# Choosing the next step by its later phases too, and the first batch ahead of the second, in a planned four-layer diffusion-transformer kernel

## What is computed

```python
# layer 0: self-attention with a 1024x1024 mask, rope; layer 1: no mask; layer 3: rope, no mask
# layer 2: self-attention in windows of 128 tokens, rolled by 64
for layer in (0, 1, 2, 3):
    h = modulate(layernorm(x), cond)                    # all tokens of a batch
    q, k, v = heads(h @ w_qkv)
    x = x + gate * (softmax(q @ k.T * 0.25 (+ mask)) @ v @ w_o + b_o)
    h = layernorm(x)                                    # modulated, but in layer 1
    q = h @ w_cross_q;  k, v = heads(ctx @ w_kv)        # 77 keys
    s = q @ k.T * 0.25                                  # layer 2: only the 16 largest scores of a row count
    x = x + gate * (softmax(s) @ v @ w_co + b_co)
    h = modulate(layernorm(x), cond)
    x = x + gate * (act(h @ w1 + b1) @ w2 + b2)         # gelu; in layer 2 silu(h @ a) * (h @ b)
```

## Time and profile before

| | us |
|---|---|
| median of 3 runs | 3243.97 (3241.6 to 3250.75) |
| the profiled execution | 3256.22 |
| its span, first to last instruction | 3254.4 |
| PE busy | 2751.2 (85%) |
| DVE busy | 1942.0 (60%) |
| ACT busy | 1529.2 (47%) |
| POOL busy | 669.2 (21%) |
| mean granted TensorE clock | 0.888 |

### The profile page before, as it was taken

How to read it: one execution, slowest core, us unless ns; L and a number is a source line. 1 busy time by engine, 2 the same in 40 slices (tenths; PEclk the granted TensorE clock), 3 DMA queues, 4 the chain that set the end, 5 groups by cost and what they waited for, 6 DMA issues and landing times.

```text
span 3254.4 us, 44342 instructions
## 1 busy us (share of the span) xinstructions
PE 2751.2 (85%) x13324; PEld 1246.8 (38%) x13376; DVE 1942.0 (60%) x4404; ACT 1529.2 (47%) x2744; POOL 669.2 (21%) x970
## 2 busy tenths in 40 slices
PE   5899999897889999998889774657688999997788
PEld 3433343224452423223546552334323523232545
DVE  6787566243458687752443567756997278873421
ACT  2055646553535575675353442323244374676242
POOL 4010100212411111112241334433312000112020
PEclk9699999888789999998889886768889999998878
DMA  5412112212441332133264652210412023124220
GB/s 182 132 55 64 47 50 83 81 35 85 125 121 44 92 113 63 51 96 101 77 178 116 190 165 74 74 32 27 127 37 52 17 63 101 47 76 127 80 92 17
DMA packets 254274, 275.88 MB, mean 85 GB/s; under 512 B 60485, under 2 KB 195424, under 8 KB 253664
## 3 DMA queue, kind: packets, MB, share of 16 engines
q1 hardware_dynamic: 242783, 271.58, 28.4%
q0 software_dynamic: 11264, 1.46, 0.3%
HBM read 157.36 MB, written 114.09 MB: 83 GB/s over the span
## 4 chain that ended last, share of the span: by engine, by line
PE 68%; DVE 13%; issue 7%; ACT 4%; DMA 4%; POOL 3%; SPq 1%; ACTq 0%; DVEq 0%; POOLq 0%
PE ring_a L1207 10%; PE ring_c L1281 10%; PE ring_b L1251 10%; PE ring_b L1304 7%; PE ring_a L1316 7%; PE ring_b L1166 4%; PE ring_a L1293 4%; PE ring_b L1250 3%; DVE row_max L1547 2%; ACT probs L1385 2%; PE ring_b L1275 2%; PE ring_b L1132 2%; PE ring_a L1180 2%; PE ring_a L1304 2%; DVE x_norm L1464 1%
## 5 line engine op out<-in xcount | busy, mean ns | idle before, releaser
L1385 ACT ACTIVATE probs<-ring_b 128x512 f32<-128x512 f32 (+1 forms) x1728 | 913.3, 600 | 569.3 <-PE ring_b L1251 469.8
L1547 DVE TENSOR_REDUCE row_max<-ring_a 128x1 f32<-128x1024 f32 x512 | 600.3, 1219 | 105.2 <-PE ring_a L1207 101.9
L1251 PE MATMUL ring_b<-q_ring,k_ring 100*128 100x512 bf16 x1536 | 525.5, 387 | 36.4 <-ACT probs L1385 22.8
L1207 PE MATMUL ring_a<-k_ring,q_ring 96*128 96x512 bf16 x1536 | 492.8, 410 | 45.8 <-DVE row_max L1547 20.2
L1281 PE MATMUL ring_c<-probs,v_and_ones 128*17 128x512 f32 x3072 | 410.0, 606 | 3.4 <-ACT probs L1385 3.4
L1665 POOL CAST neg_max_parts<-neg_max 16x128 bf16<-16x128 f32 x112 | 35.6, 318 | 1804.0 <-ACT neg_max L1379 1476.7
L1544 DVE CUSTOM_DVE_ANT_0 w_mlp<-ring_a,w_mlp 128x1024 bf16<-128x1024 f32 x256 | 304.1, 1222 | 82.9 <-PE ring_a L1207 80.0
L1591 DVE TENSOR_TENSOR x_tok<-x_tok,ring_a 128x512 f32<-128x512 f32 x96 | 66.0, 687 | 413.8 <-PE ring_a L1316 260.1
L1207 PEld LDWEIGHTS ring_a<-k_ring,q_ring 96*128 96x128 bf16 x1536 | 125.9, 100 | 405.4 <-issue 333.9
L1251 PEld LDWEIGHTS ring_b<-q_ring,k_ring 100*128 100x128 bf16 x1536 | 146.7, 99 | 312.4 <-issue 207.2
L1304 PE MATMUL ring_b<-h_feat,w_mlp 128*128 128x512 f32 x512 | 247.6, 633 | 8.7 <-ACT h_feat L1350 8.6
(11 more groups left out here) (138 smaller groups left out, 3319.3 us busy)
## 6 DMA issues: line engine op xcount, KB each, us to landing
q_ring<-scr_q SPq DMA_DIRECT2D x128, 384.0 KB, 4.0
scr_q<-split SPq DMA_DIRECT2D x64, 384.0 KB, 3.1
k_ring<-scr_k SPq DMA_DIRECT2D x64, 384.0 KB, 4.8
scr_q<-split SPq DMA_DIRECT2D x64, 256.0 KB, 3.2
scr_out<-out_stage SPq DMA_DIRECT2D x128, 128.0 KB, 2.5
scr_out<-out_stage SPq DMA_DIRECT2D x64, 256.0 KB, 2.0
h_feat<-scr_out SPq DMA_DIRECT2D x56, 256.0 KB
reciprocals<-scr_recip SPq DMA_DIRECT2D x56, 256.0 KB
```

The lines of the kernel that those rows point to most:

```text
L1207: last = mm(ps[:, half * BLOCK:(half + 1) * BLOCK], q[0:PARTS, h, t * P:(t + 1) * P], k_view(g)[0:PARTS, h, half * BLOCK:(half + 1) * BLOC ...
L1251: last = mm(ps[:, :], k_view(g)[0:ROWS, h, s.kt * P:(s.kt + 1) * P], q[0:ROWS, h, q0:q0 + BLOCK], start=not g.masked, stop=True)
L1385: f(PT[0:n, s.pt, :], ps[0:n, :], ACT.Exp, **kw).then_inc(b_evac, 1)
L1547: v.tensor_reduce(NM[:, s.nm, s.u:s.u + 1], ps, AX.X, ALU.max).then_inc(a_evac, 1)
```

## The change

No operation is added or taken away: 5254 steps of the same kinds and counts stand in both lists. What changes is the planner that orders them:

- `run()` looks at the later phases of the step it has chosen: where a ready step of lower rank has that phase's engine as its own first engine and could begin within `YIELD[engine]` of the time at which the phase would start, that step is taken in its place.
- Ranks go by layer, and batch 2 has `LATER` = 8.5 added to every rank. Ranks within a batch run from 0 to 9, so batch 1 comes first in nearly every choice.
- The second pass of self-attention waits in the plan until its v is there.
- `REACH`, the planned latency behind an engine (`LINK`, one for each engine now), and nearly all planned durations are other numbers. `DELAY` of batch 2 is 200, but it bears on none of the threads that a network starts, which begin at 0.

```diff
-LINK = 0.15
+LINK = dict(PE=0.22, ACT=0.16, DVE=0.13, POOL=0.12, SP=0.1)
...
     def emit(self, s, at):
         for n, (eng, us) in enumerate(s["ph"]):
-            at = max(at, self.free[eng]) if n == 0 else max(at + LINK, self.free[eng])
-            if eng == "ACT" and "fn" in s and s["fn"] != self.table:
+            at = max(at, self.free[eng]) if n == 0 else max(at + LINK[s["ph"][n - 1][0]], self.free[eng])
+            if s["kind"] in ("root", "ctx_root"):
+                self.table = "exp"
+            elif eng == "ACT" and "fn" in s and s["fn"] != self.table:
                 self.table = s["fn"]
                 us += 1.3
...
             at, t = min(((at, t) for at, t in ready if t.want["ph"][0][0] == eng and at <= first + REACH[eng]),
                         key=lambda x: (x[1].rank, x[0]))
+            for n, (eng, us) in enumerate(t.want["ph"][1:]):
+                before = at + sum(u for _, u in t.want["ph"][:n + 1]) + LINK["PE"]
+                begins = max(before, self.free[eng])
+                ahead = [(o.rank, a, o) for a, o in ready
+                         if o.want["ph"][0][0] == eng and o.rank < t.rank and a <= begins + YIELD[eng]]
+                if ahead:
+                    _, at, t = min(ahead, key=lambda x: x[:2])
+                    break
...
-REACH = dict(PE=0.25, ACT=5, DVE=0.8, POOL=0.15, SP=2)
-DELAY = [8.0, 60.0]
...
+REACH = dict(PE=0.15, ACT=0.1, DVE=1.2, POOL=0.35, SP=0.5)
+YIELD = dict(ACT=0, DVE=-0.5, POOL=-0.5, PE=0.5)
+DELAY = [8.0, 200.0]
+LATER = [8.5, 8.5, 8.5, 8.5]
+
+
+def rank_of(kind, l, b, blk):
+    return (RANK[kind][l] + LATER[l] * b, l, b, blk)
...
-            root = yield do("root", [("ACT", 0.6)], after=[s], counts=["root_n"], fn="exp", l=l, b=b, blk=blk, of=s)
+            root = yield do("root", [("ACT", 2.95)], after=[s], counts=["root_n"], l=l, b=b, blk=blk, of=s)
...
+            if n == 0 and not st.cross:
+                yield ("flag", key + ("v",))
```

More of the change, by code:

```diff
@@ L285, in split_chain @@
             r3 = None
-        s = yield do("project", [("PE", 1.85 * (0.6 if ck else 1)), ("ACT", f * (0.7 if rope else 1.4))],
+        s = yield do("project", [("PE", 1.75 * (0.6 if ck else 1)), ("ACT", f * (0.6 if rope else 1.2))],
                      after=[h, w, raw_last, sp_last, r3], ring="b", counts=["proj"], l=l, b=b, cross=cross,
@@ L488, in firsts @@
             units = PAIR * TILES if kind == "full" else PAIR
-            pe, dve = (0.45, 1.31 if g.masked else 1.22) if kind == "full" else (0.85, 0.85 if kind == "cross" else 1.25)
+            pe, dve = {"full": (0.43, 1.22 if g.masked else 1.14), "window": (0.45, 1.14), "cross": (0.34, 0.73)}[kind]
             for u in range(units):
@@ L523, in seconds @@
                 for tile, (qt, pt_last) in enumerate(places):
-                    pe = 0.43 if (kind == "full" and g.masked) else 0.45 if kind == "window" else 0.22
-                    s = yield do("score", [("PE", pe), ("ACT", 0.6)], after=[g.max_put, m, pt_last], ring="b", g=g, kt=kt, fn="exp",
+                    pe = 0.44 if (kind == "full" and g.masked) else 0.26 if kind == "window" else 0.22
+                    s = yield do("score", [("PE", pe), ("ACT", 0.58 if g.edge else 0.49)], after=[g.max_put, m, pt_last], ring="b", g=g, kt=kt, fn="exp",
                                  tile=tile, pt=qt, pt_last=pt_last)
@@ L552, in products @@
                     ost, o_last, o_uses = yield ("get", "OST")
-                    ph = [("PE", 4.0 if kind == "window" else 1.05), ("ACT", 0.65)]
+                    ph = [("PE", 2.4 if kind == "window" else 0.99), ("ACT", 0.5)]
                     s = yield do("pv", ph, after=unit.scores + [v, c_last, o_last], ring=None if kind == "full" else "b",
```

94 lines of the change are left out of this document (47 added, 47 removed).

## The result

The changed kernel takes 3314.0 us (median of 4 runs, 3303.0 to 3316.2), the kernel before beside it 3243.5 (4 runs, 3241.6 to 3250.8). The ratio is 1.021, with a 95% interval from 1.018 to 1.023. The change makes the kernel slower by 2.1%, where 3.9% faster was forecast. The profiled execution took 3314.6 us, its span is 3312.8; it is read against the 3254.4 of before.

A forecast was written before the change was run, and what follows sets the result against it. PE was taken to bound the attentions; elsewhere chains over several engines and HBM are waited for. Terms -15 - 30 + 20 + 20 - 110 + 10 - 21 = -126 gave execution 3130, times 0.9962: 3118 us, range 3040 to 3235.

The forecast's parts named there:

- layer 1 to the end of the top-k: From layer 1's last `pv` through the top-k: work moved under attention saves 110 us, ends -160 and -25.
- The 170: Last `pv` of layer 1 to the first top-k mark: 170 us, taken between 150 and 191 for 139 of work.
- The 139 for batch 2's ten units: Top-k of layer 2: batch 2's first 10 units, with little beside them, take 139 us at 13.8 each.
- All of batch 2's units at 20.4 us: Top-k of layer 2: if batch 2's units take as long as before, the term of -110 becomes -25.
- Start and layer 0, -15: Up to the end of the masked attentions: 15 us saved where 570 to 733 lost 40, between -25 and +10.
- Layer 0 to 1, -30: Layer 0's last `pv` to layer 1's first `first`: 150 us instead of 230, net -30, ends -60 and +10.
- Switches, +20 and +20: Between the batches' attentions in layers 1 and 3: new losses of 20 us each, ends 0 and 45 each.
- layer 3's cross-attention, +10: Batch 1's cross-attention of layer 3, mixed with batch 2's self-attention: 10 us lost, ends -5 and +55.
- The end, -21: Last `pv` to the end: only batch 2's chain remains, 175 us instead of 273, net -21, ends -45 and +15.
- The clock comes back: Rival, mixed stretches: PE's clock at 0.95 or more saves 60 to 90 us more, 3030 to 3050; chance 0.12.
- The new losses eat the gain: Rival: upper-end switch losses (+50) and batch 2's top-k at 20.4 us a unit (+85), 3190 to 3253; chance 0.14.
- "slower" rival: Mixed attention, about 800 us of work: early batch 1 steps block PE's queue, 145 us lost, to 3262; chance 0.12.

The follow-up runs named there:

- e5: The changed kernel with strict precedence of batch 1 in layer 0 alone, `LATER = [8.5, 0, 0, 0]`: 3286.2 us, ratio 1.012.
- e13: The changed kernel with its own durations and a precedence of two ranks in layer 0 only, `LATER = [2, 0, 0, 0]`: 3261.1 us, ratio 1.005.
- e10: The changed kernel with strict precedence of batch 1 in layers 0 and 1 alone, `LATER = [8.5, 8.5, 0, 0]`: 3307.9 us, ratio 1.019.
- e1: The changed kernel with no precedence of batch 1 in any layer, `LATER = [0, 0, 0, 0]`: 3268.9 us, ratio 1.007.
- e9: The changed kernel with strict precedence in layers 0 to 2 and none in layer 3, `LATER = [8.5, 8.5, 8.5, 0]`: 3299.9 us, ratio 1.017.
- e14: The changed kernel, strict precedence kept, its planner counting PE steps 4%, HBM trips 0.5 us and passes between engines 0.05 us longer: 3327.6 us, ratio 1.026.
- e8: The changed kernel, its planner counting PE steps 8% and HBM trips 1 us longer, with `LATER = [2, 0, 0, 0]`: 3210.6 us, ratio 0.989.
- e7: The kernel before with only the durations, table rule and `LINK` of the changed kernel: 3346.5 us, ratio 1.030.
- e11: The kernel before with `LINK` = 0.14 in place of 0.15 and nothing else different: 3266.1 us, ratio 1.006.
- e17: The kernel before with only the strict precedence, 8.5 added to the ranks of batch 2: 3374.1 us, ratio 1.038.
- e18: The kernel before with only the look-ahead at a step's later phases: 3378.4 us, ratio 1.040.
- e6: The changed kernel, strict precedence kept, its planner counting every HBM trip 1 us longer: 3298.9 us, ratio 1.015.

## Why the prediction was wrong

*The total.* 3118 was forecast, 3314 came, outside the range of 3040 to 3235; the step that failed is the sum's main term, **-110** for "layer 1 to the end of the top-k". It measured 966 us from the last `pv` of layer 1 to the last transposition, where 833 was built (979 before): 133 of the 189 us, while layer 3's attention came as forecast. The price of the 170 in it, a rate of work for a stretch in which a chain is waited for, is the part that cost most.

*The 170.* It was made of work: 139 us at a rate between 1.08 and 1.38. The forecast itself had noted a chain there, "over `out`, norm, cross-attention and the context", but gave it no length of its own, as it did for the end. Doing so with the end's terms (22 + 9 + 24 + 8 + 24 + 15 + 9 and an MLP block of 30) gives 141 before any wait of its own or the loads of q; with what those terms measured at the end (27, 9, 24, 15, 33, 25, 5 and 30) it is 168, and HBM trips that took 7 to 9 us come on top. A rate read off a stretch that has much other work in it didn't hold once that work was gone. Before, 1502 to 1931 lost 117 of 429 us; now 107 are lost in 244. The work went, the loss stayed. But it needn't all have stayed: e5 and e13, without precedence in layer 1, take 208 and 203 us with the same work. So about half of the miss on the 170 is the chain that had no price, and about half came with the precedence in layer 1. That it does so by batch 1's steps standing ahead of batch 2's chain is argued from the chain above, not shown.

*The 139 for batch 2's ten units.* The period of 13.8 us is that of a batch with nothing more important beside it. Batch 1's units kept it (217 us for 16). Batch 2's yield to every step of batch 1, and went at 19.6; with the precedence of layer 2 gone they went at 14.7 (e10). From first to last mark batch 2's units took 370 us in the changed kernel, 284 without precedence (e1) and 258 with two ranks in layer 0 (e13). As a place this was right, as a price of the kernel's time it wasn't: e10 is no faster than e9.

*An end of the range.* "All of batch 2's units at 20.4 us" was given as -25. Sixteen units at 20.4 are 327 us, less than the 350 that the sum holds for them; the ten built at 13.8 would add 66, so the rival with both losses would stand at 3234 and not at 3253.

*Start and layer 0, -15.* +12 came, just outside its ends. The mixture at 563 to 745 lost 18 us, less than the 25 forecast, and its clock was 0.99 where the like of it before had 0.84; the loss of 107 to 563 was 59 instead of 43.

*Layer 0 to 1, -30.* 174 instead of 150, within the ends given for it. The MLP blocks came as built and the first `up` 11 us earlier; the way from `down` to `first`, with the cross-attention and projections in it, took 104 where 68 were built.

*Switches, +20 and +20, and layer 3's cross-attention, +10.* These held: 27 and 23 by the rows above, and 535 against 531 for the stretch behind.

*The end, -21.* 202 instead of 175. The chain was the right idea. The forecast showed no rows for three of its terms (22, 8 and 15), and these measured 27, 15 and 25; the fourth, 24, measured 33.

*Rivals.* "The clock comes back" did not: the mean clock is 0.884, against 0.888 before. In this trace 563 to 745, 91% busy, has 0.99 and 1610 to 1854, 72% busy, has 0.78. The Trainium skill, "TensorE: Matmul & The Clock Gate", section "What's actually happening", has activity release the throttle. These two rows agree; 570 to 733 before, 90% busy at 0.84, agrees in part only. "The new losses eat the gain" named the slow units of batch 2, though not the +74. The "slower" rival had the right sign with the wrong mechanism: it wanted mixed attention to lose 25% of its length, and layer 1's lost 13% (691 us with 639.16 busy at 0.94), with PE at 9 tenths as the forecast asked. The rival that was missing is the one of the experiments: a strict order between two batches costs time by itself, 45 us here. Two ways in which it does are seen. With precedence in layer 1, the first mark comes later behind the last `pv`, with the same work between them (e10 against e5). And batch 1 can use up the attention that batch 2's chains need for cover (e14). The question of what is left for batch 2 once batch 1 is ahead was not asked.

*What was not asked.* The prediction valued each moved block where it landed and never asked whether the order as a whole was better. That order could be laid out from the kernel's own durations, and it came out 20 us worse than the old one: the right sign, though less than a third of the 70 us.

*What stays open.* Why the look-ahead and the durations help among the new ranks and hurt among the old ones was not taken apart; neither were the new ranks, the reaches and the wait for v alone. The 18 to 26 us by which the change without strict precedence is slower than before (e13, e1) have no cause of their own shown. The estimates from laid-out orders were 17 to 52 us too low for the changed rules from e5 on (e8 aside, which came as estimated) and 11 to 24 too high for the old ones (e7, e11, e17, e18), so they miss something, and they don't rank kernels closer than about 30 us.

## What to carry to other kernels

A stretch in which a chain is waited for needn't get shorter in proportion when its other work is moved away: give the chain a length of its own, trip by trip, and take that as the floor. With two independent streams on one machine with in-order queues, don't rank one strictly ahead of the other without a test: here it cost 45 to 123 us under three sets of rules, while two ranks in the first layer or none came out within 10 us of each other. A longer stretch is not yet a loss: look at what was done in it (the top-k of e9 and e10). A greedy order is a draw: change an irrelevant number before believing a gain, and lay the new order out with given durations before building it.

## What the runs showed of the hardware

One execution of e6 took 10253.5 us; the three others of the same kernel took 3288.5 to 3305.3. In the profile of that one the mean granted clock is 0.23 and PE is busy for 9981.9 of 10251.7 us, while DVE's busy time (1967.1) is near the usual one. ACT's busy time is higher, but the mean exponential (L1403) takes 597 ns, against 604 in the changed kernel. A mean matmul of `score` (L1269) takes 1276 ns, against 387. So only TensorE was slow, from the second slice of 40 to the last. Its granted clock there is neither 1.0 nor 0.5, the two levels of the kernel before: it is 0.16 at 512 to 5000 us and 0.26 from 7000 on. Why is not known; the other three executions had 0.88 on average.

```profile
PE 9981.9 (97%) x13376; PEld 3068.0 (30%) x13376; DVE 1967.1 (19%) x4404; ACT 1667.9 (16%) x2747; POOL 664.5 (6%) x970
PEclk8311111111111111111122222222222222222222
```

In the changed kernel a trip of the denominators to `scr_recip` or of the reciprocals back stands in the chain at 1610 to 1854 with 3.4 to 7.6 us (one piece is 1.5), the DMA engines 46% busy there, and in the chain at the end with 3.7 to 4.4, at 23%.
